# A fused attention and expert layer on one core: the order of its first projection and of the passage from its last attention cell to the experts, and one program block in place of two

## What is computed

```python
q, k, v, s = x @ Wq, x @ Wk, x @ Wv, clip(x @ Ws, -32, 32)    # by head: 64, 64, 128, 64 wide
z = cumlogsumexp(s, over time)
g, p = exp(z[t-1] - z[t]), exp(s - z)
# scan over time, for each head:
hk = hk * g + k[:, None] * p[None, :];  ok = q @ hk           # q scaled by 1/8
hv = hv * g[:, None] + p[:, None] * v;  o = softmax(ok) @ hv
o = o * rsqrt(mean(o * o) + 1e-5) * g_norm * silu(x @ Wg)
x = layernorm(x + o @ Wo)
h = relu(x @ W1 + b1);  alpha = softmax(h @ W2 + b2)          # 8 experts
out = layernorm(x + sum_k alpha[k] * ((x @ V[k].T) @ U[k].T))
```

## Time and profile before

| | |
|---|---|
| median of 3 runs | 1351.45 us (1350.58 to 1351.91) |
| the profiled execution | 1352.65 us |
| its span, first to last instruction | 1350.7 us |
| outside its span | 1.95 us |
| TensorE busy | 1328.9 us, 98% of the span |
| VectorE, ScalarE, GpSimd busy | 822.1, 472.1, 276.6 us |
| DMA | 31.73 MB |

### The profile page before, as it was taken

One profiled execution on the slowest core, in us unless ns is written; L12 is line 12 of the kernel. 1 busy time (PEld: TensorE's weight loads), 2 busy tenths in 40 slices (PEclk: granted clock), 3 DMA queues, 4 the chain that ended last, 5 costly groups with the idle time before them and its releaser, 6 DMA issues. The chain is left out here.

```text
span 1350.7 us, 20318 instructions
## 1 busy us (share of the span) xinstructions
PE 1328.9 (98%) x8144; PEld 1139.8 (84%) x8144; DVE 822.1 (61%) x1559; ACT 472.1 (35%) x1391; POOL 276.6 (20%) x254
## 2 busy tenths in 40 slices
PE   8999999999999999999999999999999999899998
PEld 6788888888888888888888888888888888778886
DVE  6556656566665565566665566666555666756754
ACT  5333433343333333333234333333333323422221
POOL 3111411132112201231114111221122111222211
PEclk9999999999999999999999999999999999999999
DMA  6000200001000100010001000010000210000010
GB/s 203 16 0 1 56 1 17 1 24 32 17 1 24 32 17 1 8 48 10 7 0 48 9 16 1 25 32 17 1 24 25 63 32 1 1 1 32 13 50 32
DMA packets 35356, 31.73 MB, mean 23 GB/s; under 512 B 7616, under 2 KB 28096, under 8 KB 35264
## 3 DMA queue, kind: packets, MB, share of 16 engines
q1 hardware_dynamic: 35264, 30.44, 7.5%
HBM read 26.24 MB, written 4.19 MB: 23 GB/s over the span
## 5 line engine op out<-in xcount | busy, mean ns | idle before, releaser
L845 PE MATMUL p<-wvg_hi,xt_hi 128*128 128x512 f32 x512 | 210.5, 411 | 0.0
L847 PE MATMUL p<-wvg_hi,xt_lo 128*128 128x512 f32 x512 | 201.5, 394 | 0.0
L846 PE MATMUL p<-wvg_lo,xt_hi 128*128 128x512 f32 x512 | 200.6, 392 | 0.0
L494 ACT ACTIVATE v_tok<-p 128x256 f32<-128x256 f32 x128 | 49.8, 389 | 339.0 <-PE p L847 339.0
L653 DVE SCALAR_TENSOR_TENSOR gate<-th,p 128x256 f32<-128x256 f32 x128 | 53.9, 421 | 173.2 <-ACT th L498 169.7
L845 PE MATMUL p<-xt_hi,wsqk_hi 128*128 128x512 f32 x380 | 148.4, 391 | 0.0
L846 PE MATMUL p<-xt_lo,wsqk_hi 128*128 128x512 f32 x380 | 148.2, 390 | 0.0
L847 PE MATMUL p<-xt_hi,wsqk_lo 128*128 128x512 f32 x380 | 147.8, 389 | 0.0
L440 POOL TENSOR_TENSOR orstd<-ovar,minus_half 128x8 f32<-128x8 f32 x32 | 52.4, 1639 | 453.3 <-DVE ovar L775 453.3
L434 POOL TENSOR_TENSOR v_lo<-v_tok,v_hi 128x256 fp32r<-128x256 f32 x96 | 84.0, 888 | 196.3 <-ACT v_hi L503 196.3
L847 PEld LDWEIGHTS p<-wvg_hi,xt_lo 128*128 128x128 f32 x512 | 96.5, 188 | 22.7
(11 more groups left out here) (213 smaller groups left out, 2846.1 us busy)
## 6 DMA issues: line engine op xcount, KB each, us to landing
raw<-in_L_attn_Wv SPq DMA_DIRECT2D x32, 128.0 KB, 2.4
raw<-in_L_attn_Wg SPq DMA_DIRECT2D x32, 128.0 KB, 2.9
raw<-in_L_attn_Wo SPq DMA_DIRECT2D x16, 256.0 KB, 2.8
out<-acc SPq DMA_DIRECT2D x16, 256.0 KB, 2.0
acc<-in_L_attn_hidden_states SPq DMA_DIRECT2D x3, 1024.0 KB, 7.4
raw<-in_L_attn_Ws SPq DMA_DIRECT2D x8, 256.0 KB, 2.9
raw<-in_L_attn_Wq SPq DMA_DIRECT2D x8, 256.0 KB, 2.9
raw<-in_L_attn_Wk SPq DMA_DIRECT2D x8, 256.0 KB, 3.1
```

Of the source, the lines that this page charges most:

```text
L494: nc.scalar.activation(v_tok[:, c, :], PB[bk][:, 0:VW], ACT.Copy).then_inc(v_done, 1)
L845: nc.tensor.matmul(out_, lh, rh, start=(k == 0), stop=False)
L846: nc.tensor.matmul(out_, lh, rl, start=False, stop=False)
L847: last = nc.tensor.matmul(out_, ll, rh, start=False, stop=(k == n - 1))
```

## The change

1. **The first projection by kinds of halves.** The four hi·hi products come first, each behind its piece of `xt_hi0` and behind the high half of Ws; then four with the low half of Ws behind `w_lo_done`; then four with `xt_lo0`. Eight transposes of the identity stand ahead of the transposes of x and eight behind them (`keep_warm`).
2. **The first cell.** ScalarE makes `e_tok_hi` and `v_hi` of chunk 0 right behind the first values (no wait for `ok_summed`), and VectorE copies the first state to `hv` ahead of pz. The low rows of Wo (`low_rows`) go to the end of the cell. At the start, ScalarE splits piece 6 of the weights behind `x_high(2)`, not ahead of it.
3. **The last two cells.** The split of W1 goes into the middle of cell 30, and there the statistics of batch 0 go ahead of the third gate, no longer just ahead of `ovar`; the blocks of V into cell 31 between its products, and x of batch 0 ahead of its last values.
4. **One block.** Attention and experts stand in one block, and the experts use the PSUM banks of attention. The first two tiles of h run while the last y is made; the blocks 4 and 5 of U and the transposes of y follow, then h tile 2, the last output rows, blocks 6 and 7 of U, h tile 3 and `vx_tile(0)`. The second statistics and the normalisation of batch 1 stand behind all that on VectorE, and on GpSimd the rstd of batch 1 stands behind the four `ht_lo`. The logits of group 0 also wait for all eight low blocks.
5. **Memory.** `v_raw` shares its place with `ut_lo`, and `w1_raw` with `w1_lo`.

```diff
+        PREP = [SB[0], SB[1], SB[0], SB[1], bank_v0, bank_v1, TB[0], TB[1]]
+        X1 = [bank_v0, TB[0], XB, bank_v1]
...
@@ cell_gpsimd
+            if cell.b == CELLS - 2:
+                for kt in range(KT):
+                    car.w1_low(pool, kt)
             pool.wait_ge(ovar_done, cell.count(1, 1))
@@ cell_scalar
             values_scalar(act, cell, 0)
+            if first(cell):
+                act.wait_ge(e_tok_done, 1)
+                slots_high(act)
+                values_high(act, cell, 0)
             values_scalar(act, cell, 1)
...
+            if last:
+                for kt in range(KT):
+                    car.x_high(act, 0, kt, X1[kt])
@@ cell_vector
                                     ALU.subtract).then_inc(ok_less_top, 1)
+            else:
+                keep_values(0)
...
                 if c == 0 and last:
+                    car.prep_low(dve, 0, PREP[0])
+                    car.prep_low(dve, 1, PREP[1])
+                if c == 1 and last:
                     car.norm1_apply(dve, 0)
+                    car.prep_low(dve, 2, PREP[2])
+                    car.prep_low(dve, 3, PREP[3])
@@ feature_proj, the first projection
+                pe.wait_ge(w_hi_done, 1)
+                for kt in range(KT):
+                    pe.wait_ge(xt_hi_done, kt + 1)
+                    nc.tensor.matmul(PB[bk][:], wsqk_hi[:, i, kt, :], xt_hi[b][:, kt, :], start=(kt == 0), stop=False)
+                pe.wait_ge(w_lo_done, i + 1)
+                for kt in range(KT):
+                    nc.tensor.matmul(PB[bk][:], wsqk_lo[:, i, kt, :], xt_hi[b][:, kt, :], start=False, stop=False)
@@ tensor_part
+            def keep_warm(n):
+                for _ in range(n):
+                    nc.tensor.transpose(TB[1][:, 0:P], ident[:], ident[:])
@@ experts, TensorE, group 0
+                if g == 0:
+                    hidden(0, 0)
+                    hidden(0, 1)
+                    car.prep_turn(pe, 4, PREP[4])
+                    car.prep_turn(pe, 5, PREP[5])
+                    att.tail_turns(pe)
+                    hidden(0, 2)
+                    att.tail_rows(pe)
+                    car.prep_turn(pe, 6, PREP[6])
+                    car.prep_turn(pe, 7, PREP[7])
+                    hidden(0, 3)
...
                 if g == 0:
                     pe.wait_ge(w2_lo_done, 1)
+                    pe.wait_ge(car.prep_lo, 2 * KT)
@@ experts, VectorE, ahead of group 0
             nc.vector.memset(w2_pad[:].bitcast(F32), 0.0).then_inc(zeroed, 1)
+            att.tail_outputs(dve)
+            car.prep_low(dve, 4, PREP[4])
+            car.prep_low(dve, 5, PREP[5])
+            att.tail_turns_low(dve)
+            att.tail_sums(dve)
+            car.prep_low(dve, 6, PREP[6])
+            car.prep_low(dve, 7, PREP[7])
@@ experts, GpSimd
-                if g < G:
+                if 1 < g < G:
                     car.norm1_rstd(pool, g)
...
+                if g == 1:
+                    car.norm1_rstd(pool, 1)
```

More of the change, by code:

```diff
@@ L214, in bank @@
         def bank(name):
[L215 removed]
+            return whole.enter_context(nc.psum_tensor(name, [P, BANK], F32))
         def sem(name):
[L218 removed]
+            return whole.enter_context(nc.semaphore(name))
         xt_hi, xt_lo = [], []
@@ L530, in cell_scalar @@
                 y_high(act, cell, 1)
[L532 to L535, removed]
+            if not first(cell):
+                act.wait_ge(ok_summed, cell.count(1, 1))
+                slots_high(act)
+                values_high(act, cell, 0)
             values_high(act, cell, 1)
@@ L700, in cell_vector, with keep_values @@
                 y_vector(dve, cell.shifted(-1))
+            def keep_values(c):
+                dve.wait_ge(hv_summed, cell.count(CH - 1, c + 1))
+                for h in range(2):
+                    rows_own = slice(h * M, (h + 1) * M)
+                    copied = nc.vector.tensor_copy(hv[rows_own, c, :], XB[rows_own, P + h * DV:P + (h + 1) * DV])
+                copied.then_inc(hv_kept, 1)
             def keep_keys(c):
@@ L743, in cell_vector @@
             for c in range(CH - 1):
[L744 to L748, removed]
+                if c > 0 or not first(cell):
+                    keep_values(c)
+                if c == 0 and cell.b == CELLS - 2:
+                    dve.wait_ge(added, CH * (CELLS - B + 1))
+                    car.norm1_stats(dve, 0)
                 if c == 0 and last:
+                    car.prep_low(dve, 0, PREP[0])
+                    car.prep_low(dve, 1, PREP[1])
+                if c == 1 and last:
                     car.norm1_apply(dve, 0)
+                    car.prep_low(dve, 2, PREP[2])
+                    car.prep_low(dve, 3, PREP[3])
                 if c < 2:
@@ L970, in cell_tensor @@
                     output_rows(pe, cell, c)
+            if last:
+                car.prep_turn(pe, 0, PREP[0])
+                car.prep_turn(pe, 1, PREP[1])
             def running_values(c):
@@ L989, in cell_tensor @@
             turned(PZ_BANK, [pz[:, c, :, :].rearrange("p h m -> p (h m)") for c in range(CH)], pz_turned)
+            if last:
+                for n in (2, 3):
+                    pe.wait_ge(car.prep_lo, n - 1)
+                    car.prep_turn(pe, n, PREP[n])
             token_proj(pe, cell, 3)
@@ L996, in cell_tensor @@
             else:
-                pe.wait_ge(gate_done, cell.count(CH, CH - 1))
-                car.prep_turn(pe, 0, PREP[0])
+                pe.wait_ge(car.prep_lo, KT)
             pe.wait_ge(pz_t_done, cell.count(1, 1))
@@ L1012, in cell_tensor @@
             else:
-                pe.wait_ge(gate_done, cell.count(CH, CH))
-                for n in range(1, KT):
-                    car.prep_turn(pe, n, PREP[n])
+                for kt in range(KT):
+                    if kt == 0:
+                        pe.wait_ge(gate_done, cell.count(CH, CH - 1))
+                    if kt == KT - 1:
+                        pe.wait_ge(gate_done, cell.count(CH, CH))
+                    car.x_turn(pe, 0, kt, X1[kt])
             pe.wait_ge(v_done, cell.count(CH, CH))
@@ L1084, in sem @@
         def sem(name):
-            return ctx.enter_context(nc.semaphore(name))
+            return whole.enter_context(nc.semaphore(name))
         sb("carried", [P, car.later_tiles, KT * D])
@@ L1330, in turn_one @@
                     elif not last:
+                        if g == 0 and k == 0:
+                            att.wait_tail_sums(pe)
                         if k >= 2:
```

237 lines of the change are left out of this document (133 added, 104 removed).

## The result

The changed kernel takes 1344.12 us, median of four runs (1342.65 to 1344.9); the kernel before takes 1351.68 beside it (1350.58 to 1352.5). The ratio is 0.9936, with a 95% interval from 0.9925 to 0.9948. So it is faster by 0.64%, with an interval clear of 1. That is 1.1 us above the forecast of 1343.0 and within its range. The profiled execution took 1344.9 with a span of 1343.2, against 1350.7: 7.5 us less.

A forecast was written before the change was run, and what follows sets the result against it. TensorE was taken as the bound, busy 1328.9 of 1350.7 us. Head 6.0 plus passage 2.5 gave 8.5 won: 1352.65 to 1344.15, less 1.2 for the median, 1343.0; range 1340.2 to 1346.2.

The forecast's parts named there:

- First projection, -1.8: Start of the kernel: the new product order ends the projection at 12.5 instead of 14.30, 1.8 us won (0 to 1.8).
- Everything behind follows 2.0 earlier.: Behind the first projection: the 1.8 won there and 0.2 from piece 6 carry on to all later work.
- First cell, -4.0 (2.9 + 1.5 - 0.4): First cell: the v_lo wait goes (2.9), token_proj 2 regains full pace (1.5), a new pz wait costs 0.4.
- Cell 30 and cell 31: Last two cells: work moved into cell 30 costs nothing; three new waits in cell 31 cost 0.3 each, 0.9 together.
- The passage, 4.0 - 1.5 = 2.5: From attention to experts: idle falls from 8.2 to 4.2, including 3.3 ahead of the logits; half pace behind costs 1.5.
- (b): Rival at the logits: the wait is short or doesn't lower the clock, 1.5 more won, 1341.5; chance 0.14.
- (d): Rival at the passage: it gives nothing, the logits wait 6 us, 2.5 lost, 1345.5; chance 0.14.
- (c): Rival at the start: the clock is low in the first projection, 1.8 lost, 1344.8; chance 0.12.
- (e): Rival in the first cell: the wait moves to pz or hv_kept, 2 us, pace falls again, 1346.1; chance 0.06.
- (f): Rival from cell 31 on: short waits keep the clock down, 84 matmuls cost 20 us, 1363; chance 0.02.
- Two at 0.44 for a first pair: Start of the trace: transposes read as running at half pace, part of the argument that transposes raise the clock.
- a low clock below 15 us: Start of the kernel: a sign that would show the prediction wrong.

The follow-up runs named there:

- second set of runs: The changed kernel and the kernel before, both run again unchanged on another chip: 1344.07 against a median of 1352.63 us.
- x1_first: Changed kernel with ScalarE's copies of x of batch 1 ahead of its copy of piece 3 of the weights: 1343.97 us.
- head_only: Kernel before with the start and first cell of the changed kernel, its last cells and two blocks as before: 1347.18 us, ratio 0.9962.
- after_again: The changed kernel run again unchanged, as the measure for the other runs: 1344.07 us, ratio to before 0.9935.
- three_orders: Changed kernel with w2_pad early, x of batch 1 copied ahead of piece 3, first-cell k transposes awaiting only their bank's low half: 1338.12 us, ratio 0.9895.
- no_warm: Changed kernel without its 16 added transposes of the identity: 1345.52 us.

## Why the prediction came out as it did

The forecast was right by its size, and most of its steps by theirs. One term, the start, was far too large, and that the total still came so close is in part luck: in the second set of runs the gain is 8.6 against 8.5 forecast, with this term wrong by 0.6 to 1.6 us.

- **First projection, -1.8.** -1.44 in the trace. The low half of Ws and the last `xt_hi` came 0.2 later than assumed (9.99 instead of 9.79), and the hi·hi products, at 0.43 apart while they wait for ScalarE, end 0.2 later still. The mechanism was half named: the order alone, without the transposes, ends at 14.60. "The other 16 transposes lie in idle time" is true of their cost and silent on their use.
- **"Everything behind follows 2.0 earlier."** This step failed. It is worth 0.42 in the profiled pair at the end of the slot scores (their last row starts at 36.85, before at 37.27), and 0.4 to 1.4 by all runs. The prediction looked for what could be late behind the first projection and named x of batch 1; what was late was piece 3 of the weights, on ScalarE ahead of the copies of batch 1, 3.4 us behind the new end. In the trace before, its copy stood at 15.76 and hid behind the late projection. Of the queues behind the moved step only TensorE's and the DMA of x had been followed, not ScalarE's.
- **Piece 6, -0.2.** Not to be seen apart; behind it the `xt_lo` wait ahead of k's transposes is 0.27, and 1.16 in x1_first.
- **First cell, -4.0 (2.9 + 1.5 - 0.4).** Right: 4.35 in the trace, 3.99 by undoing it. The three terms came as 2.89, 1.4 to 1.6, and 0.16 instead of 0.4, as `keep_values(0)` fitted beside exp.
- **Cell 30 and cell 31.** No wait in cell 30; the 1.0 at 1151 is gone; cell 31 has 0.2 and 0.2 where 0.3 each was assumed.
- **The passage, 4.0 - 1.5 = 2.5.** In the trace 9.20 - 4.93 = 4.27 and -1.7, so 2.6; by the runs 3.1 (1347.18 - 1344.1), a difference into which the clock's fall at the end of head_only, 0.85 in its trace, may enter. The wait of 3.3, its releaser `w2_pad` and the half pace behind it came as forecast. Rivals (b) and (d) fall: the wait is neither short nor 6 us.
- **Sum.** 8.5 predicted. 4.8 + 2.6 = 7.4 of it in the traces (spans: 7.5), 7.6 between the first medians, 8.6 in the second set. The distance of the median from the profiled execution, -1.2, was -0.8 this time. Rivals (c), (e) and (f) fall as well: the products behind 10.99 ran at full pace, pz took 0.16, and no short wait lowered the clock.
- **Two readings.** "Two at 0.44 for a first pair" is not half pace: such a pair took 0.63 to 0.69 at half pace and 0.44 at full pace. The fall from 0.42 to 0.27, on which the argument rests, is read rightly. And in rival (f) half pace doesn't cost 0.236 more for a matmul: the starts stand 0.43 apart where they stand 0.23 apart at full pace, so it is 0.2, and the 84 matmuls would have cost 17 us and not 20.
- **What would show it wrong** also named "a low clock below 15 us". The granted clock reads 1.00 there in every window, but in after_again and three_orders the transposes of x run at half pace until 8 and recover only within the second eight: the sign looked for would have missed it, the lengths show it.

## What to carry to other kernels

When a stage is made to end earlier, go through every engine's order from that point and ask of each instruction what its own start was tied to: a copy that waits for a DMA, ahead of the one you need, takes the gain, and it can't be seen in the trace before because the late stage hid it. A small operation that a long wait hangs on is to be put where its input is ready, and not where it is used: one of 0.19 us, moved ahead of 7 us of statistics and normalisation, was worth 4.6 to 5.1 us, more than the whole rebuilt passage. Where the order couldn't be mended, filling the 3.3 us of idle time ahead of a run of matmuls with transposes into a free bank was worth 0.9 to 1.4. And a gain read from one pair of traces should be read at several places along the way: here equal cells alone differ by 0.9 us between executions.

## What the hardware showed

- Idle time of 2.9 us (three traces) and 3.3 (six traces) was followed by half pace each time. After 2.1, at the step between the blocks, the clock stayed at 1.00 in both traces of the kernel before, but fell in head_only, which has the same 2.1 us wait there. This is its window:

```profile
1175.00:1180.00 5.00, 4.96 (x18) 4.31 (x19) 4.19 (x7) 1.79 (x3) 2.73 (x3) 0.50 0.00 0
```

  So the length of one idle time does not decide it alone.
- How soon the pace comes up at the start differs between executions of one kernel: in the changed one after 5.0 us in the first trace and within the second eight transposes, past 8.2, in the second; in the kernel before at 7.0 and at 12.4. This is a part of the scatter of 1.3 to 4 us that these kernels show, and the variants whose logits don't run at half pace have less of it (0.4 to 1.1).
- The granted clock is no guide at the start: in no_warm it reads 1.00 from 10 to 12 and from 12 to 14, where the products stand 0.43 apart; in the first trace of before it reads 0.59 and 0.55 there, at nearly the same distance. The distance of the starts shows the pace in both.
- The same VectorE operation takes longer where GpSimd works beside it: four operations of the normalisation take 1.92 here and 3.84 in the earlier trace rows, the low half of `w2_pad` 0.19 against 1.26, pz 0.69 against 1.13.
